# Wider exponentials in the rotary attention stage, and a router moved forward into it

## The reference, cut to what matters

```python
# rotary attention: B, S, H, Dh = 4, 1024, 16, 8
scores = einsum('bhqd,bhkd->bhqk', rope(q), rope(k)) / sqrt(Dh)
out = einsum('bhqk,bhkd->bhqd', softmax(scores), v) @ Wo + bo
# depth feed-forward, on x = layernorm(x + out)
weights = (x @ w_r + b_r).squeeze(-1)                   # the router: one number for a row
threshold = top_k(weights, 512)[0][:, -1]
selected = weights > threshold                           # about half of the 1024 rows
blk = gelu(x @ W1 + b1) @ W2 + b2                        # 128 -> 512 -> 128
out = where(selected, blk, x)
```

## Time and profile before

| | |
|---|---|
| median of 3 runs | 1837.24 us (1831.24 to 1838.89) |
| the profiled execution, its own time | 1837.1 us |
| its span (first to last instruction) | 1835.3 us |
| mean granted TensorE clock | 0.974 |
| first rotary exponential starts, last one ends | 1204.5, 1723.9 us |
| ending, from there to the end of the span | 111.4 us |

### The profile page before, as it was taken

The page is one execution under the profiler, slowest core; times in us unless marked ns, Lnnn a source line. Parts: engine busy times, 40 slices in busy tenths (PEclk is TensorE's granted clock), DMA queues, the critical chain, the costliest instruction groups (busy, mean ns, idle before and its releaser), DMA issues. The chain is left out here.

```text
span 1835.3 us, 29249 instructions
## 1 busy us (share of the span) xinstructions
PE 1668.2 (91%) x10754; PEld 885.7 (48%) x10754; DVE 1106.1 (60%) x1905; ACT 1276.1 (70%) x2453; POOL 891.4 (49%) x621
## 2 busy tenths in 40 slices
PE   7898589999999999999999999789999999898975
PEld 4565455555555555655555554323333333232354
DVE  4679669787688887787876666523314133020296
ACT  4554136867667666867586757678899999999733
POOL 3455456887766778666887678730000000000033
PEclk8999799999999999999999999979999999999988
DMA  3000221212111111111111211130312213101001
GB/s 83 2 12 2 103 88 56 84 59 67 55 46 41 60 55 45 55 45 55 45 57 43 62 38 35 46 116 24 116 46 93 69 47 99 63 24 38 1 12 37
DMA packets 38790, 97.55 MB, mean 53 GB/s; under 512 B 5040, under 2 KB 16496, under 8 KB 38512
## 3 DMA queue, kind: packets, MB, share of 16 engines
q1 hardware_dynamic: 38640, 95.59, 16.7%
HBM read 49.96 MB, written 28.84 MB: 43 GB/s over the span
## 5 line engine op out<-in xcount | busy, mean ns | idle before, releaser
L1133 POOL TENSOR_TENSOR b_psum<-b_psum,b_probs 128x1024 f32<-128x1024 f32 x192 | 460.0, 2396 | 216.1 <-ACT b_probs L1293 209.8
L2589 ACT ACTIVATE c_probs<-banks 128x1024 f32<-128x1024 f32 x512 | 483.6, 1030 | 38.7 <-PE banks L2638 23.5
L1293 ACT ACTIVATE b_probs<-banks 128x1024 f32<-128x1024 f32 x256 | 255.4, 1022 | 217.7 <-PE banks L1439 217.4
L1649 DVE TENSOR_TENSOR b_gated<-banks,b_g 128x480 f32<-128x480 f32 x512 | 310.8, 653 | 137.7 <-PE banks L1404 129.1
L1404 PE MATMUL banks<-b_w,b_xh 128*128 128x480 f32 x1024 | 353.4, 398 | 37.2 <-ACT b_probs L1293 15.2
L1665 DVE TENSOR_REDUCE b_tok<-b_gated 128x192 f32<-128x960 f32 x248 | 272.3, 1138 | 0.3
L1262 ACT ACTIVATE b_share<-b_o,b_picked 128x64 f32<-128x64 f32 x1080 | 269.1, 341 | 1.7 <-DVE b_o L1690 1.7
L2652 PE MATMUL banks<-c_probs,c_vg 128*32 128x512 f32 x2048 | 249.8, 605 | 2.9 <-DVEq L2703 2.6
L1404 PEld LDWEIGHTS banks<-b_w,b_xh 128*128 128x128 f32 x1024 | 194.8, 190 | 118.7 <-issue 59.8
L1474 PE MATMUL banks<-b_probs,b_tok 128*64 128x512 f32 x1024 | 248.2, 605 | 2.6 <-ACT b_probs L1293 2.6
L1439 PE MATMUL banks<-b_qq,b_kk 64*128 64x512 f32 x1536 | 228.3, 421 | 5.9 <-DVE b_gated L1649 5.4
(11 more groups left out here) (268 smaller groups left out, 1827.2 us busy)
## 6 DMA issues: line engine op xcount, KB each, us to landing
b_w<-b_split_w SPq DMA_DIRECT2D x24, 960.0 KB, 4.7
b_kk<-b_kk SPq DMA_DIRECT2D x64, 256.0 KB, 3.6
c_heads<-c_split SPq DMA_DIRECT2D x24, 512.0 KB
c_keys<-c_heads SPq DMA_DIRECT2D x16, 512.0 KB, 3.9
c_queries<-c_heads SPq DMA_DIRECT2D x16, 512.0 KB, 4.8
b_split_w<-b_w SPq DMA_DIRECT2D x8, 960.0 KB, 6.0
b_raw_w<-in_L_ffn_W SPq DMA_DIRECT2D x8, 480.0 KB, 4.1
c_heads<-c_split SPq DMA_DIRECT2D x8, 384.0 KB
```

The costliest lines, as they stand in the source:

```text
L1133: nc.gpsimd.tensor_tensor(psum[:, par, :], prev, probs[:, i % 4, :], ALU.add).then_inc(psum_rdy, 1)
L1293: nc.scalar.activation(probs[:, i % 4, :], score_b[i % 2], ACT.Exp).then_inc(exp_rdy, 1)
L1649: nc.vector.tensor_tensor(shape(gated[:, t % 2, j, :]), shape(proj_b[u % WAYS][:, 0:HALF_W]), g.unsqueeze(2).broadcast_to([P, 3, HD2, E]), ...
L2589: nc.scalar.activation(probs[:, step % 4, c, :, :], unit_b[u % NU], ACT.Exp, scale=float(HD) ** -0.5).then_inc(exp_rdy, 1)
```

## The change

Two things change.

1. In the rotary stage a unit is three tiles (`WIDE` = 3) in three banks, and two units (`NU` = 2) rotate over banks 0 to 5. An exponential is 128 x 1536. There are 342 units, the last of one tile. `probs` becomes a ring of 15 tiles, and an exponential waits until the products of the tile 15 places back are done. TensorE's loop goes by units: the products of pair p stand behind the scores of the second unit after the one that holds the pair's last tile, and `between` (the turn or the piece of the pair) stands ahead of the scores of the next such unit.
2. The router of batches 0 to 2 (the batches whose r3 is ready) moves into the rotary stage of batches 1 to 3, as four more pieces (`router_turn`, `router_row`, twice) at steps 47, 49, 53 and 55, with VectorE's part (`column`, `rank`, `choose`) at steps 56 to 61. The column is made there by VectorE with the identity and a sum, without TensorE. The two small router loads are issued earlier. In the ending only batch 3 has a router; `expand(b + 1, 0)` is put ahead of `contract(b)`, and `norm(3)` no longer stands behind `choose(0)`.

```diff
-    NU = 3
-    PIECE_STEPS = [i for i in range(5, STEPS * NG, 2) if i % NT != TURN][:NE + NX]
+    D_PIECES = [("router_turn", 0), ("router_row", 0), ("router_turn", 1), ("router_row", 1)]
+    NU, WIDE, RING = 2, lead.WIDE, lead.RING
+    TILES = B * BS * G
+    UNITS = -(-TILES // WIDE)
+    PIECE_STEPS = [i for i in range(5, STEPS * NG, 2) if i % NT != TURN][:NZ + NX + ND]
+    RANK_AT, RANK_STEPS = 57, NT + 4
...
-                act.wait_ge(pv_done, ONE + STEPS - 3 + step)
-                for c in range(2):
-                    nc.scalar.activation(probs[:, step % 4, c, :, :], unit_b[u % NU], ACT.Exp, ...)
+                n, slot = len(tiles_of(u)), WIDE * u % RING
+                spent = tiles_of(u)[-1] - RING
+                if spent >= 0:
+                    act.wait_ge(pv_done, ONE + STEPS + spent // G + 1)
+                act.wait_ge(score_ps, ONE + u + 1)
+                nc.scalar.activation(probs[:, slot:slot + n, :], unit_b[u % NU][:, 0:n, :], ACT.Exp, ...)
...
+            def first_unit(pair):
+                return -(-(2 * G * (pair + 1)) // WIDE) + 1
+            pair = 0
+            for u in range(UNITS):
+                score_unit(u)
+                if u == first_unit(pair):
+                    for step in (2 * pair, 2 * pair + 1):
+                        products(step // BS, step % BS)
+                    pair += 1
+                if pair and u + 1 == first_unit(pair):
+                    between(2 * pair + 1)
...
+            def column(b):
+                dve.wait_ge(used, d_index(b, ND))
+                st.link(nc.vector.tensor_tensor(own, w_row..., ident..., ALU.mult))
+                st.link(nc.vector.reduce_sum(w_col[:, :], own, AX.X))
+            def rank(b, part):
+                for t in range(2 * part, 2 * part + 2):
+                    st.link(nc.vector.tensor_scalar(ge, w_row[:, :], w_col[:, t:t + 1], None, ALU.is_ge, ALU.add, accum_out=count[:, t:t + 1]))
...
             turn_x(0)
             next(left, None)
-            router_row(0)
             next(left, None)
-            router_column(0)
+            expand(0, 0)
             for b in range(B):
-                expand(b, 0)
...
-                if b + 1 < B:
+                if FIRST <= b + 1 < B:
                     router_row(b + 1)
...
                 expand(b, 3)
+                if FIRST <= b + 1 < B:
+                    router_column(b + 1)
                 if b + 1 < B:
-                    router_column(b + 1)
+                    expand(b + 1, 0)
                 contract(b)
```

More of the change, by code:

```diff
@@ L2517, in pieces, with tiles_of, units_for @@
                 at.update({PIECE_STEPS[(NE if first else NZ) + k]: (x_index(b + 1, k), kind, half, b + 1) for k, (kind, half) in enumerate(X_PIECES)})
-            return at
+            if not first:
+                at.update({PIECE_STEPS[NZ + NX + k]: (d_index(b, k), kind, half, b - 1) for k, (kind, half) in enumerate(D_PIECES)})
+            return at
+        def tiles_of(u):
+            return range(WIDE * u, min(WIDE * (u + 1), TILES))
+        def units_for(tiles):
+            return -(-tiles // WIDE)
         def turned_at(b, i):
@@ L2667, in _, with between @@
             pe.wait_ge(used, NX)
-            def batch(b, first, last):
-                at = pieces(b, first, last)
-                for i in range(BS):
-                    step = b * BS + i
-                    score_unit(step, 1)
-                    if step + 1 < B * BS:
-                        score_unit(step + 1, 0)
-                    if i % 2 == 0 and step:
-                        for back in (2, 1):
-                            products(*((b, i - back) if i else (b - 1, BS - back)))
-                    if i % NT == TURN and not (first and i == TURN):
-                        turn(*((b, i // NT - 1) if i > TURN else (b - 1, NP - 1)), (NX if first else z_index(b, 0)) + sum(j < i for j in at))
-                    if i in at:
-                        piece(*at[i], turned_at(b, i))
-            score_unit(0, 0)
-            batches(pe, batch)
-            for back in (2, 1):
-                products(B - 1, BS - back)
+            def between(step):
+                b, i = step // BS, step % BS
+                at = pieces(b, b == 0, b == B - 1)
+                if i % NT == TURN and step > TURN:
+                    turn(*((b, i // NT - 1) if i > TURN else (b - 1, NP - 1)), (z_index(b, 0) if b else NX) + sum(j < i for j in at))
+                if i in at:
+                    piece(*at[i], turned_at(b, i))
+            def first_unit(pair):
+                return -(-(2 * G * (pair + 1)) // WIDE) + 1
+            pair = 0
+            for u in range(UNITS):
+                score_unit(u)
[5 more added lines that the diff above has]
+                    between(2 * pair + 1)
+            while 2 * pair < B * BS:
+                for step in (2 * pair, 2 * pair + 1):
+                    products(step // BS, step % BS)
+                pair += 1
             def left():
@@ L2713, in piece @@
                     tail.take(dve, half, bank).then_inc(used, 1)
-                elif kind == "turn_x":
+                elif kind in ("turn_x", "router_turn"):
                     nc.vector.tensor_copy(xT[:, cols], bank).then_inc(used, 1)
+                elif kind == "router_row":
+                    if half == 0:
+                        dve.wait_ge(weights.r_in, 16 * 2)
+                    nc.vector.tensor_scalar(w_row[:, cols], bank, weights.br[:, 0:1], None, ALU.add).then_inc(used, 1)
                 elif kind == "turn_out":
@@ L2777, in batch @@
                         norm(b - 1)
+                    if i == RANK_AT - 1 and not first:
+                        column(b)
+                    if RANK_AT <= i < RANK_AT + NT // 2 and not first:
+                        rank(b, i - RANK_AT)
+                    if i == RANK_AT + NT // 2 and not first:
+                        choose(b)
                     if i == TAIL_NORM and first:
```

181 lines of the change are left out of this document (117 added, 64 removed).

## The result

The changed kernel takes 1846.6 us (median of 5 runs, 1844.9 to 1848.3), before it stood at 1837.2 beside it: ratio 1.0054, 95% interval 1.0034 to 1.0074. It is slower by half a per cent, where I had forecast 1829, and lies just outside the range of 1815 to 1845. The profiled execution has a span of 1844.5 us.

The account below looks back on a forecast made before the run. ScalarE and TensorE were both taken as nearly the bound in the rotary stage, TensorE's waits as the ending's limit. Span 1835.3 + 15 (rotary stage) - 22.9 (ending) = 1827.4, about 1829 us executed; forecast 1823 to 1835, range 1815 to 1845.

Parts of the forecast that it names:

- The ending: After the rotary stage: TensorE's new order laid end to end at full clock, -22.9 us, between -18 and -25.
- The exponentials: ScalarE in the rotary stage: an instruction of 1.45 us, starts 1.33 apart, 3.56 us a pair against 3.91.
- The pairs with a long piece: Rotary stage: TensorE becomes the bound, 4.13 us a pair against 3.91; 42 such pairs, +9.2 us.
- rival B: Rotary stage loses only 0 to +8 us, as three-unit pairs' slack takes long pieces; 1820 in all, chance 0.22.
- The router's part in the rotary stage: VectorE's counts, column and choice hide in eight steps, 15.4 us in 15.6; the router loads too: zero.
- The plain pairs: Rotary stage, 84 pairs without a long piece: 3.87 to 3.90 us against 3.91, taken as -1 us.
- each pair is about 0.31 late: Rotary stage: the exponential after the products' block starts at 4.31, ScalarE free at 4.00; a pair takes 3.87 us.
- in the same lateness: Rotary stage: the ring of 15 adds a wait once in three pairs, but inside the 0.31 us lateness.
- The norms: Layer norms in the rotary stage: TensorE's 1.86 us wait gets through to ScalarE, +1.2 us each, +3.6 for three.
- C: Rival: two units too few, extra lateness shows in every pair; 1855 from 0.2 us a pair, chance 0.13.
- A: Rival: ScalarE sets the rotary stage's pace, the 0.31 us lateness doesn't show; 1793 in all, chance 0.06.
- the Trainium skill's rule: Larger operations help a saturated engine; otherwise breaking them up can help; by its first half the stage wins 0.35 a pair.

Follow-up runs that it names:

- run 4: The changed kernel with a ring of 18 tiles and no wait for the products ahead of an exponential: 1827.9 us, ratio 0.9942, rotary stage 535.0.
- run 1: Only the new units, ring and order against the kernel before, the router of all four batches left in the ending: 1868.9 us, ratio 1.0192.
- run 3: Only the router moved, old two-tile units in three buffers, products wait only at every second exponential as in the kernel before: 1814.3 us, ratio 0.9876.
- run 5: The changed kernel with a ring of 18 tiles, the wait ahead of every exponential kept: 1842.7 us, ratio 1.0041, rotary stage 543.5.
- Run 7: The changed kernel with four unused transposes in each pair without turn or piece: 1840.3 us, ratio 1.0010, rotary stage 542.0.
- Run 6: The changed kernel without the layer norms of batches 0 to 2 in the rotary stage, a copy instead: 1842.5 us, ratio 1.0018.
- run 8: The changed kernel with units of two tiles, still in two buffers, ring of 16: 2099.9 us in one execution, rotary stage 805.9.
- run 2: Only the router moved, old two-tile units in three buffers, with the products wait ahead of every exponential: 1822.45 us, ratio 0.9930, rotary stage 529.5.

## Why the prediction was wrong

*The ending* was right in mechanism and size: -23.9 against -22.9. The first contract starts 16.8 us after the last exponential instead of 20.2, and from there to the end of the last one it takes 53.4 where 54.3 was worked out; `choose(3)` fitted.

*The exponentials* were right: 1.45 us, 1.33 to 1.35 apart. By the Trainium skill (ScalarE: Activation LUTs, What ACT_TABLE_LOAD costs) an estimate for 1536 columns is 186 + 0.833 x 1536 = 1466 ns; the trace has a median of 1450 and agrees within 1.1%.

*The pairs with a long piece* look right and aren't. 12.39 was worked out for three pairs (3 x 4.13), with TensorE as the bound in all 42, and 12.46 is measured without the extra wait (run 4), 12.57 with it. But 12.46 is the time of any three pairs with a long piece in the short gap, also when the two others have none, and 11.98 the time of three pairs with two long pieces and a turn in the short gap. So TensorE isn't the bound over three pairs: the two other places take a long piece for nothing, as rival B had it ("long pieces fall in pairs that have three units, where the slack takes them"), and the place with two units pays for all. 14 of the 42 groups of three pairs have one there.

*The router's part in the rotary stage* at nothing was right (run 1: 551.3 without, 551.9 with; run 3: 518.2 with, 519.4 without).

*The plain pairs* were the step that failed, together with the clock below. The prediction had them "at 3.87 to 3.90 against 3.91". They take 4.03 (12.10 for three), or 3.96 with an empty short gap. The exponential was put 0.50 + 0.03 behind its scores; it starts 0.61 behind them. About 0.06 of that is the second wait in front of it, which the diff shows (`act.wait_ge(pv_done, ...)` now ahead of every exponential) and which I priced at nothing. Run 3 shows its cost in the old order, 0.19 us for three pairs, and run 4 against 5 in the new, 0.12. That "each pair is about 0.31 late" was wrong in its even spread too. Without the wait (run 4) two of three pairs are 0.33 late; the third, with the short gap, isn't late at all if it is empty, and 0.62 late behind a turn. The ring's wait was said to fall "in the same lateness". That was right except with an empty short gap: it shows as idle time of 14.5 us of its own, but takes the place of another wait (12.10 us for three pairs in both, run 5).

*A term that was missing* is TensorE's clock. I looked at it in the ending and took full clock for the rotary stage. It spends 30.7 us at half clock instead of 3.4, and TensorE is idle for 67 us of the stage instead of 40. Run 7 ties the one to the other: with unused work in the idle time it is 10.2 us at half clock and 0.44% faster. Without the wait and with 18 places (run 4) the half-clock time is 6.8. So 17 us of the 32.5 are the wait and the ring with the clock stretches that come with them, and 15.6 are the units.

*The 535.0 of run 4* against the predicted 534.4 is partly luck. Its 15.6 us more than before are made up otherwise than the 15 of the sum. The norm of batch 1, done in batch 2, costs 5 where three norms were to cost 3.6 together, and the two others nearly nothing; long pieces in the short gap cost 7 instead of 9.2; turns and short pieces there cost 3.6 and empty gaps give back 1.9, where -1 stood for all plain pairs; the rest is in the first 75 us and the end.

*The norms*, at 1.2 us each, were too small for one of the three: in batch 2 TensorE's wait was 4.16 us, not 1.86, because VectorE's eight normalizing instructions took 4.17 us there, where they mostly take 2.1. One of the eight took 2.37 us, the others 0.34; the same happened at the same place in runs 1, 4, 5 and 7, and not in run 3. The trace shows what it met. GpSimd's `c_xb` (1522.19, 2.40 us) starts 0.11 us before that instruction, and the instruction ends 0.08 us after it. Over all kernels here 17 normalizing instructions start while this GpSimd instruction runs, and all 17 take 2.26 to 2.39 us, up to its end; the 55 copies from PSUM to SBUF that start under it take their usual 0.68 to 0.69. In the kernel before it starts at 1507.30, when the last of the eight (1507.15 to 1507.49) is already running, and holds nothing. The three-tile order moved the norm against GpSimd's work, a collision that the prediction had no term for. No run moved one of the two on purpose. Run 6, without norms, puts all three at 5 to 8 us.

*The rivals.* C came nearest in kind: extra lateness in the loop has no buffer, deciding at 0.14 a pair. What came is 17 / 128 = 0.13 on average, but as 0.06 in two of three pairs and the rest mostly by the clock. It had a chance of 0.13, and its sources were named too narrowly (a slower exponential); the diff itself held a source. Of B the mechanism holds for two of three places, and its 0 to +8 us don't. A didn't come: no pair stands at 3.6. Of the Trainium skill's rule (Perfetto Trace Analysis, Optimizing Scalar/DVE Operations) the second half fits the direction: ScalarE was busy 86% of the stage, and the larger operation came with more idle time on TensorE. But it isn't shown by itself. Smaller operations with three buffers (run 3) are 17 us faster in this stage than the best wide ones with two (run 4), while smaller ones with two (run 8) are 254 us slower than the changed kernel, so the number of buffers decides.

## What to carry to other kernels

Before widening an instruction by giving up a buffer, lay the longest block that the feeding engine can't interrupt against the finished work that is left in the buffers, and count every instruction between release and start, waits that are long over too. In a loop without slack 0.06 us at one instruction a pair was most of half a per cent of the kernel (run 2 against 3). If the units don't divide the period of the loop, walk through the whole period: here a piece was free in two places of three and cost up to 1.1 us in the third. And when a change adds waits to TensorE, price its clock as well.

When a change has two parts that meet two limits, run each alone: one saved 24 us in the ending and cost nothing in the stage that it moved into, the other cost 32.

## What wasn't expected of the hardware

A semaphore wait that is already satisfied, placed ahead of the wait that counts, delayed a ScalarE instruction by 0.06 us (0.541 to 0.603 us after the scores' matmul with units of 1024 columns, 0.550 to 0.610 with 1536; medians of the late exponentials in runs 3, 2, 4 and 5).

A VectorE instruction from SBUF to SBUF that started under a GpSimd instruction from SBUF to SBUF was held until that one ended, 2.3 us instead of 0.34, in 17 of 17 cases; copies from PSUM under the same instruction were not.

More work made TensorE's stage faster: about 0.58 us of unused transposes in otherwise light pairs took the half-clock time from 30.7 to 10.2 us. With two buffers of two tiles the stage went to a mean granted clock of 0.79.

In run 2 eight exponentials, 32 steps apart (steps 11, 43, 75 and so on), came 0.47 us late instead of 0.19: 0.88 us after their scores' matmul, where the others take 0.60. They are gone in run 3. What holds ScalarE there is open.
